# Graph network kernel: six of thirteen layer-1 products moved between the groups of the next tile's aggregation

## The reference

```python
# layer 0
t1 = feat @ W1
msg = t1[src] + feat[src] * feat[dst] @ W2
msg = msg / (sqrt(out_deg[src]) * sqrt(out_deg[dst]))[:, None]
embed = where(in_cnt > 0, t1 + segment_sum(msg, dst), 0) + b
embed = leaky_relu(embed, 0.01); embed = embed / max(norm(embed), 1e-12)
# layer 1
norm = dinv[row] * ew * dinv[col]
h7 = segment_sum((h @ W)[col] * norm[:, None], row) + b
out = relu(h7 @ W1 + b1) @ W2 + b2
```

## Time and profile before

| | us |
|---|---|
| median of 3 runs | 2332.73 (2323.42 to 2341.97) |
| profiled execution, own time | 2324.01 |
| its span, first to last instruction | 2322.1 |
| TensorE busy | 1936.2 (83%) |
| VectorE busy | 1340.0 (58%) |
| GpSimd busy | 1082.0 (47%) |
| ScalarE busy | 487.8 (21%) |
| granted TensorE clock, mean | 0.896 of 2.4 GHz |

### The profile page before, as it was taken

One profiled execution on the slowest core, in us unless ns is written; L12 is line 12 of the kernel. 1 busy time (PEld: TensorE's weight loads), 2 busy tenths in 40 slices (PEclk: granted clock), 3 DMA queues, 4 the chain that ended last, 5 costly groups with the idle time before them and its releaser, 6 DMA issues. The chain is left out here.

```text
span 2322.1 us, 23042 instructions
## 1 busy us (share of the span) xinstructions
PE 1936.2 (83%) x7229; PEld 1169.0 (50%) x7239; DVE 1340.0 (58%) x1970; ACT 487.8 (21%) x636; POOL 1082.0 (47%) x1561
## 2 busy tenths in 40 slices
PE   5499587767777767667669999999989999999996
PEld 1188422254544444445446776677874344434443
DVE  7977598823323322223224555566568777878885
ACT  1000200033333223223325545330043000000000
POOL 1888888887888888888886000000004000000000
PEclk9755588988988888889889999999999999999998
DMA  7888830035334535433444775238724555655663
GB/s 275 333 326 325 323 125 16 1 97 186 116 114 169 172 114 175 151 128 134 150 150 169 258 253 189 80 103 309 226 68 123 158 163 164 186 168 153 171 180 105
DMA packets 338570, 394.92 MB, mean 170 GB/s; under 512 B 114000, under 2 KB 319674, under 8 KB 325563
## 3 DMA queue, kind: packets, MB, share of 16 engines
q1 hardware_dynamic: 219593, 306.93, 38.4%
q10 hardware_dynamic: 93110, 86.22, 11.2%
q0 software_dynamic: 25792, 0.88, 0.9%
HBM read 221.43 MB, written 172.51 MB: 170 GB/s over the span
## 5 line engine op out<-in xcount | busy, mean ns | idle before, releaser
L377 POOL DMA_INDIRECT table<-valT,idxT x806 | 809.7, 1005 | 158.9 <-issue 157.6
L2005 PE MATMUL psum<-wgt,big 128*65 128x384 f32 (+3 forms) x1600 | 530.1, 493 | 1.0 <-DVE wgt L1953 1.0
L1953 DVE SCALAR_TENSOR_TENSOR wgt<-ratio,l3q,fcj 128x768 f32<-128x768 f32 (+2 forms) x400 | 412.1, 1046 | 94.6 <-PE psum L2005 86.4
L789 PE MATMUL psum<-hx,region 128*128 128x257 f32 x1250 | 336.5, 417 | 123.8 <-issue 65.0
L2005 PEld LDWEIGHTS psum<-wgt,big 128*65 128x65 f32 x1600 | 219.7, 138 | 302.8 <-issue 298.7
L789 PEld LDWEIGHTS psum<-hx,region 128*128 128x128 f32 x1250 | 247.2, 208 | 179.2 <-issue 77.9
L789 PE MATMUL psum<-region,g 128*128 128x512 f32 (+1 forms) x672 | 305.6, 599 | 16.2 <-DVE big L592 13.4
L592 DVE TENSOR_TENSOR big<-big,psum 128x512 f32<-128x512 f32 (+1 forms) x325 | 210.4, 665 | 148.2 <-PE psum L789 125.0
L375 POOL MEMSET rest<- 128x256 f32 x722 | 237.0, 328 | 48.7 <-issue 48.0
L1000 POOL PARTITION_ALL_REDUCE edges<-edge x1 | 0.5, 517 | 495.2 <-DVEq L1369 495.2
L789 PEld LDWEIGHTS psum<-region,g 128*128 128x128 f32 x672 | 129.9, 206 | 154.7 <-issue 109.8
(11 more groups left out here) (218 smaller groups left out, 1671.6 us busy)
## 6 DMA issues: line engine op xcount, KB each, us to landing
table<-tk SPq DMA_DIRECT2D x25, 3200.0 KB
fcj<-counts SPq DMA_DIRECT2D x150, 384.0 KB, 3.5
tk<-table SPq DMA_DIRECT2D x25, 1664.0 KB
counts<-region ACTq DMA_DIRECT2D x25, 1600.0 KB
tk<-table SPq DMA_DIRECT2D x25, 1536.0 KB
fcj<-counts SPq DMA_DIRECT2D x50, 448.0 KB, 3.7
counts_t<-region ACTq DMA_DIRECT2D x25, 800.0 KB
counts_b<-region ACTq DMA_DIRECT2D x25, 800.0 KB
```

What stands on the lines that cost most here:

```text
L377: eng.indirect_dma_start(out=table, out_offset=bass.IndirectOffsetOnAxis(idxT[:, c:c + 1], 0), in_=valT[:, c, :], in_offset=None).then_inc ...
L789: mm = lambda o, l, r_, st, sp: eng.matmul(o, l, r_, start=st, stop=sp, skip_group_check=True)
L1953: eng.scalar_tensor_tensor(out=wgt[:, n % NW, u, 0:w], in0=rb[:, 2 * i + u, t0 * P:t0 * P + w], scalar=qs[:, k, 2 * i + u:2 * i + u + 1], ...
L2005: last = eng.matmul(acc[p % 2][u][0:FW, b, 0:hi - lo], ftx[:, k, 2 * i + u, :], wgt[:, n % NW, u, lo:hi], start=k == 0, stop=k == NT - 1, ...
```

## The change

`EARLY` = 6. In step k TensorE computes chunks 0 to 5 of tile k-1 two at a time after the groups 3, 4 and 5 of tile k's aggregation; VectorE adds these six to the accumulator before it turns to `q`. After `q` come chunks 6 to 8, `turn_ab`, then (new place) the transposes of the first three groups of tile k+1 (`begin`), the dense product, and chunks 9 to 12. In the last two steps `begin` stays at the end, and chunks 9 and 10 stand in its place. ScalarE makes `wt` straight behind `normal`, ahead of groups 3 and 4, and copies the counts into bf16 and issues their DMA ahead of `abT`. No operation is added or removed.

```diff
@@ DVE step
                 if prev and cur:
                     eng.wait_ge(sem("wt"), prev[0] + 3)
                     itself(row(wt, prev[0]))
+                    for n in range(EARLY):
+                        lift(n)
...
                 if prev:
-                    for n in range(5 if last else 13):
+                    for n in range(EARLY if cur else 0, EARLY + 2 if last else 13):
                         lift(n)
...
-                    fill(5, 6)
+                    fill(8, 9)
...
-                    fill(7, 8)
+                    fill(10)
...
-                    fill(9, 10, 11, 12)
+                    fill(11, 12)
@@ ACT step
                 if prev:
                     normal(prev[0], g1)
-                take(k, 3)
-                take(k, 4)
-                if prev:
                     eng.wait_ge(sem("ag"), 13 * prev[0] + 1)
                     eng.activation(wt, tk[:, prev[1], :, :, 1], ACT.Copy).then_inc(sem("wt"), 1)
-                take(k, 5)
-                take(k, 6)
+                for g in range(3, 7):
+                    take(k, g)
...
-                eng.wait_ge(sem("abt"), k + 1)
-                eng.activation(abT[:, :, :].rearrange("p c n -> p (c n)"), pab, ACT.Copy).then_inc(sem("abfree"), 1)
                 if prev:
                     eng.wait_ge(sem("cb_out"), 16 * k)
                 eng.activation(cb, cs, ACT.Copy).then_inc(sem("cb"), 1)
                 eng.wait_ge(sem("cb"), k + 1)
                 eng.sem_inc(sem("pass"), 1)
                 eng.dma_start(counts_b[bass.ds(k, 1), :, :, :].rearrange("a p j d -> (a p) j d"), cb).then_inc(sem("cb_out"), 16)
+                eng.wait_ge(sem("abt"), k + 1)
+                eng.activation(abT[:, :, :].rearrange("p c n -> p (c n)"), pab, ACT.Copy).then_inc(sem("abfree"), 1)
@@ PE step
+                ending = cur and isinstance(cur[0], int) and cur[0] >= NT - 2
...
                         if g + 3 < 7:
                             turn(k, s, g + 3)
+                        if prev and g in (3, 4, 5):
+                            if g == 3:
+                                eng.wait_ge(sem("g1"), prev[0] + 1)
+                                eng.wait_ge(sem("diag"), prev[0] + 1)
+                            gathered(range(2 * g - 6, 2 * g - 4))
                     mul.then_inc(sem("q"), 1)
...
+                def begin():
+                    eng.wait_ge(sem(f"tk{1 - s}0"), 16 * (r + s) + 16)
+                    for g in range(3):
+                        turn(k + 1, 1 - s, g)
...
                 if prev:
-                    gathered(range(0, 3))
+                    gathered(range(EARLY, EARLY + 3))
                 turn_ab()
-                if prev:
-                    gathered(range(3, 5))
+                if not ending:
+                    begin()
+                elif prev:
+                    gathered(range(EARLY + 3, EARLY + 5))
                 dense()
                 if prev:
-                    gathered(range(5, 13))
-                if not last:
-                    eng.wait_ge(sem(f"tk{1 - s}0"), 16 * (r + s) + 16)
-                    for g in range(3):
-                        turn(k + 1, 1 - s, g)
+                    gathered(range(EARLY + 5 if ending else EARLY + 3, 13))
+                if ending and not last:
+                    begin()
```

More of the change, by code:

```diff
@@ L38 @@
 FIRST_CODE, LATER_CODE = 28, 112
+EARLY = 6
 assert NG * G == EC and P % GS == 0 and SH % SB == 0
@@ L860, in step, with gathered @@
             def step(cur, prev, last=False):
+                ending = cur and isinstance(cur[0], int) and cur[0] >= NT - 2
+                def gathered(chunks):
+                    j, z = prev
+                    of, g = (wt, g1) if cur else (tk[:, 0, :, :, 1], hk)
+                    for n in chunks:
+                        eng.wait_ge(sem("af"), 13 * j + max(n + 1, 3))
+                        if n < 12:
+                            mul = mm(pL[:, n % 3, :], g[:, n % 2 * P:n % 2 * P + P], of[:, 4 * (n // 2):4 * (n // 2) + 4, :], True, True)
+                        else:
+                            for o in range(2):
+                                mul = mm(pL[:, 0, o * P:o * P + P], g[:, o * P:o * P + P], of[:, NT - 1, :], True, True)
+                        mul.then_inc(sem("ag"), 1)
                 if cur:
@@ L873, in step @@
                             turn(k, s, g + 3)
-                    mul.then_inc(sem("q"), 1)
-                def gathered(chunks):
-                    j, z = prev
-                    of, g = (wt, g1) if cur else (tk[:, 0, :, :, 1], hk)
-                    for n in chunks:
-                        eng.wait_ge(sem("af"), 13 * j + max(n + 1, 3))
-                        if n < 12:
-                            mul = mm(pL[:, n % 3, :], g[:, n % 2 * P:n % 2 * P + P], of[:, 4 * (n // 2):4 * (n // 2) + 4, :], True, True)
-                        else:
-                            for o in range(2):
-                                mul = mm(pL[:, 0, o * P:o * P + P], g[:, o * P:o * P + P], of[:, NT - 1, :], True, True)
-                        mul.then_inc(sem("ag"), 1)
+                        if prev and g in (3, 4, 5):
[3 more added lines that the diff above has]
+                            gathered(range(2 * g - 6, 2 * g - 4))
+                    mul.then_inc(sem("q"), 1)
+                def begin():
+                    eng.wait_ge(sem(f"tk{1 - s}0"), 16 * (r + s) + 16)
+                    for g in range(3):
+                        turn(k + 1, 1 - s, g)
                 def turn_ab():
@@ L898, in dense @@
                     mul.then_inc(sem("e"), 1)
-                if prev:
+                if not cur:
                     eng.wait_ge(sem("g1"), prev[0] + 1)
                     eng.wait_ge(sem("diag"), prev[0] + 1)
-                if not cur:
                     gathered(range(13))
```

## The result

| | before | after |
|---|---|---|
| median | 2333.74 (4 runs beside after's) | 2364.18 (2357.88 to 2367.49, 4 runs) |
| profiled execution, own time | 2324.01 | 2357.88 |
| start of the loop (first counts) to 17 tiles later | 757.0 | 751.4 |
| the next seven tiles | 188.1 | 225.8 |
| from the last counts to the loop's end | 30.5 | 36.1 |

The ratio of the medians is 1.0128, with a 95% interval of 1.0095 to 1.016: slower by 1.3%.

What follows compares the result with a forecast made beforehand. TensorE's late results bound tiles during the scatters (until 1262 us), TensorE itself those behind. During, +5 counted as +4; with +39 behind, +43 on 2324.01 makes 2367, said as 2368; range 2300 to 2400.

Steps and rivals of the forecast that it cites:

- Behind the scatters: Tiles after the scatters end: ScalarE's order makes TensorE wait, +5.5 us per tile, +39 us in all (26 to 56).
- Wait at group 3: Behind the scatters, TensorE stands 3.5 us in every tile, as ScalarE makes `wt` before copying group 3.
- Clock: Behind the scatters, TensorE's clock may fall after the pause: +1.7 us if in every tile, 0 if never, 0.7 taken.
- Dense product: Behind the scatters, ScalarE's DMA issue ahead of `abT` makes TensorE stand 0 to 3.2 us, 1.3 taken.
- The step before the last: Near the loop's end: it loses 2 to 3 us, as its transposes stand at the end.
- Last tile: Loop's end: loses about 3.4 us, as six chunks that covered layer 0's tail now lie before `q`.
- During the scatters: Loop up to 1262 us: -17 us in late tiles and +22 in prompt ones, +5 in all (-59 to +70).
- 22 us lost in four tiles with prompt signals: During the scatters, four tiles without late signals pay as those behind the scatters do: +22 us (14 to 32).
- the count of instructions for each period of GpSimd: During the scatters, TensorE's results come out 12 instructions per three GpSimd periods, 4.4 us, however early the work is issued.
- rival 1: During the scatters every bubble goes, 5 us less in 13 tiles; losses behind stand: 2332, no change; chance 0.26.
- Rival 2: During the scatters chunks pass between groups, a tile falls by 9 us or more, to 42: 2294; chance 0.16.
- rival 3: During the scatters the backlog worsens, +3 us in 13 tiles and +12 in four, 87: 2427 in all; chance 0.08.

Runs made afterwards that it cites:

- d_act_only: The kernel before with ScalarE's two new orders alone, TensorE and VectorE as before: 2277.26 us, 1.0348 to the kernel before.
- c_begin_back: The changed kernel with `begin` at the end in every step, chunks 9 and 10 in its place: 2211.7 us, 1.0045 to the kernel before.
- a_wt_back: The changed kernel with ScalarE copying groups 3 and 4 ahead of `wt` again: 2214.43 us, 1.005 to the kernel before.
- e_act_undone: The changed kernel with both of ScalarE's new orders undone: 2344.65 us, 1.0093 to the kernel before.
- f_no_stall: The changed kernel with ScalarE's order of before, `begin` at the end, early chunks behind groups 4, 5 and 6: 2321.28 us, 1.0006 to the kernel before.
- k_begin_early: f_no_stall with `begin` ahead of the dense product, as in the changed kernel: 2218.96 us, 1.0079 to the kernel before.
- j_no_rest: The kernel before with no memset between scatters from scatter 28 on: 2735.57 us in one run.
- h_after: The changed kernel run again without an edit, in a series with late signals: 2349.54 us, 1.0133 to the kernel before.
- series 1 and 2: Two sets of follow-up runs; the kernel before took 2202.89 us in the first (prompt signals), 2321.29 in the second (late signals).
- b_abt_back: The changed kernel with `abT` copied ahead of the bf16 counts and their DMA again: 2221.64 us, 1.0095 to the kernel before.

## Why the prediction was right

The measured median, 2364.18, lies 3.8 us from the predicted 2368. That this is so near is luck in part. The sum was +43 and was added to the profiled execution of before, 2324, which lay 9 us under the median of before; the median rose by 30.4 (against 2333.74), the profiled execution by 33.9. In the profile the two parts of the sum missed in opposite directions: what lies behind the scatters was 4 us too low, and everything else, +4 in the sum, came out at -9.5.

**Behind the scatters: +43.3 measured, +39 forecast.** The seven intervals to the last counts took 37.7 us more (225.8 against 188.1), the end of the loop 5.6 more. Term by term:

- Wait at group 3: forecast 3.5, measured 3.3 to 3.4 in every tile, in five of six put down to ScalarE's copy, as the forecast said (once to "issue"). TensorE busy 87%, forecast under 90%.
- Clock: 0.7 was taken between 0 and 1.7; it fell in five of six tiles, which makes 1.4 in the mean, and once more in the dense product of the second, 0.25 in the mean. This is the term that was mis-sized: the trace had a fall after 3.6 us and none after 2.03, and 3.3 went with the former. (The length of the pause alone doesn't tell: in `d_act_only` the clock fell after 1.99 us, in `c_begin_back` it held after 1.97.)
- Dense product: 1.3 taken between 0 and 3.2, measured 0.86 in the mean, 0 in three tiles and 3.41 at most. The two terms are probably not independent: the fallen clock delays TensorE's own want of `abT` by as much as it costs, and so hides the issue; where it held, the next `abT` was waited for (1.35). That is read from one tile. `a_wt_back` shows the converse: less wait at group 3, and 2.8 us in front of the dense product.
- Together 3.35 + 1.4 + 0.25 + 0.86 = 5.9; the six tiles took 32.8 in the mean (196.9 by 6) against the 26.9 of before, 5.9 more. Forecast +5.5. Of its signs one missed by a tile: 30.5 to 35 us between two counts, and one tile took 37.2.
- The step before the last: forecast 2 to 3, measured 2.2. Last tile: forecast 3.4, measured 5.6. The clock, left out there, has a part: behind a pause of 3.29 us it was 0.53, and the last 28 products took 13.1 us instead of the 11.5 of before.

The cause was named as ScalarE's order with the earlier `begin`. `d_act_only` shows that the order alone is enough to make both waits; `e_act_undone` shows that without it half of a tile's loss stays (30.1 against 32.6 and 26.9); `f_no_stall` shows that with `begin` back and the chunks one group later nothing stays. From kernel to kernel, one part at a time, the loss of a tile comes apart: ScalarE's two orders 2.5 us (32.6 to 30.1), the chunks behind groups 3 to 5 instead of 4 to 6, where they wait for `diag`, 1.4 (30.1 to 28.7 in `k_begin_early`), the early `begin` 1.7 (28.7 to 27.0). The parts depend on their order: with the rest of the change in place, `wt` alone gives back nothing (`a_wt_back`). The chunks' place by itself costs nothing once what they wait for is there. The prediction named the first and the last of these three; the wait for `diag` it saw only hidden behind group 3.

**During the scatters: −5.6 measured, +5 forecast, bounds −59 and +70.** The total is near, the working is not. It foresaw 13 tiles at 49 to 51 us with `q` 6 us late or more, and 22 us lost in four tiles with prompt signals. In the result's trace `q` was 2.3 to 5.5 us late in 13 tiles, 0.2 us or less in four; the 13 took 47.9 us in the mean against 48.0 before, the four 32.3 against 33.2. So the 22 us lost in the prompt tiles did not appear, as far as four tiles tell, and the late tiles stayed as they were instead of gaining 17. The tiles took between 24.5 and 53.7 us, seventeen in 751.4. The arrivals remained late, as in this tile of the changed kernel, where ScalarE takes the transposes of `ab` 3.0 us after their end at 1159.89 (1159.23 + 0.66):

```profile
1159.23 0.66 PE L903 MATMUL psum<-ident,ab 128*128 128x128 f32 x4 [0.25 <-issue]
...
1162.91 0.60 ACT L777 ACTIVATE abT<-psum 128x512 f32<-128x512 f32 x1 [10.66 <-remote]
```

The step that failed is the count of instructions for each period of GpSimd (12 in three): `j_no_rest` refutes it as a law (306 instructions beside 489 scatters), and so does the stretch from 130 to 220 us in the trace of the kernel before (8.6 for each scatter), on which the prediction could have tried it. The conclusion drawn from it, that filling TensorE's holes there is worth next to nothing, is open. For it: the result's 751.4 us, and `f_no_stall`, 752.5 us where before takes 753.6. Against it: 713.4 and 713.6 us in the traces of `h_after` and `e_act_undone`. Their 12 and 13 late tiles take 45.3 and 44.9 us instead of 48.0. That is 3 us less for each, between the forecast (1.3 less) and rival 1 (5 less), and the 40 us gained are what rival 1 adds up to (43); with its loss behind the scatters, the one execution of `h_after` that was profiled took 2330.84, where rival 1 said 2332. So rival 1 was wrong for the result and not far from that execution. Rival 2 (42 us for a late tile, under 2310 in all) and rival 3 (87 us lost there) were not seen in any trace. The 40 us lie within the forecast's bounds, but not within its working. What the Trainium skill's page Perfetto Trace Analysis (Per-engine timelines) says of a matmul's computed end fits the arrivals 2.3 to 5.5 us behind the shown ends; that these holes were no room for work at all the runs don't show.

On the clock, the Trainium skill's page TensorE: Matmul & The Clock Gate (HAM oscillation) was cited for the other side, holes filled and so a higher clock. During the scatters the granted clock went from 0.88 to 0.89; behind them the change made new pauses of 3.3 us and it went from 1.00 to 0.94. The trace agrees with the rule, in that the clock is lower where TensorE pauses; the change made pauses where there had been none.

Left open: why the signals are prompt in one series and late in another, for the same kernel (series 1 and 2 name the same chip), and why the first 17 tiles of the same changed kernel take 751 us in one execution with late signals and 713 in another. Whether the place of the buffers or anything else that could be set has a part in it wasn't tried. The prediction took the late signals of the one trace as a property of the kernel. In a prompt series the same change costs 0.5%, not 1.3%.

## What to carry to other kernels

An engine that is busy 21% can still set the pace: look at what is queued behind each of its long instructions (a copy of 3 us, a DMA issue that holds it for 4 to 8 us) in the stretch where the bounding engine has no holes, before moving them. Work moved into a hole gains only if the hole is room; where an engine's results are taken late by all who wait for them, its idle time may not be (here the same kernel gained 6 us in one execution and 40 in another, which one trace would have hidden). Compare two traces over the same number of tiles, and take a second trace of each before calling a difference of 1% a cause. When a wait is removed, work out which is next, as `a_wt_back` shows, and see whether a later gate absorbs the gain or loss before multiplying it by the number of tiles.

## What the runs showed of the hardware

- While GpSimd issues indirect DMAs in a row, TensorE's signals can come late. With 0.49 us between two of them `q` was taken 0.2 us after its last product in two series (but for a few tiles), and 2 to 8 us after it in most tiles of two other series; with 0.72 us it was prompt in the one run made (in a prompt series). With 0.30 us VectorE waited 21 us for a product in `j_no_rest`, but at most 0.9 us in another stage of the kernel before (130 to 220 us). So the gap has a part and isn't the whole of it.
- One kernel has two levels of time, medians of 2203 and 2205 us in two series, 2321 and 2334 in two others.
- With late signals the first 17 tiles of one kernel took 751.4 us in one execution and 713.4 in another (`after`, `h_after`); those of the kernel before took 757.0 and 753.6.
- A DMA issue on ScalarE of the same 800 KB held the engine for 3.1 to 7.8 us in the six tiles of the changed kernel behind the scatters. There it starts 7.5 to 8.0 us behind the issue of the tile's 1600 KB of counts on the same engine and ends 11.1 to 15.7 us behind it. In `b_abt_back` it starts over 15 us behind the counts where TensorE bounds, and holds the engine for 0.34 us. During the scatters an issue that starts as early was often short too (0.34 us).
- After a pause of 3.3 to 3.4 us TensorE's next eight products took 3.3 to 3.8 us in five tiles and 2.0 in the sixth: the same pause, not always the same clock. After 1.99 us they took 3.69 (`d_act_only`, at 811.76 us, granted clock 0.53), after 1.97 us 2.01 (`c_begin_back`, at 694.33).
